# A graph network kernel on one core: the per-block sum of the messages as four accumulating fp32 products, and two PSUM tiles of counts

## The reference, cut to what matters

```python
node_feat = _mlp(x, W_node, b_node, g_node, beta_node)
edge_feat = _mlp(edge_attr, W_edge, b_edge, g_edge, beta_edge)
row, col = (edge_index[0], edge_index[1])
message = jnp.concatenate([x[row], x[col], edge_feat], axis=1)
message = _mlp(message, W_msg, b_msg, g_msg, beta_msg)
agg = jax.ops.segment_sum(message, col, num_segments=node_feat.shape[0])
```

## Time and profile before

| | us |
|---|---|
| median of 3 runs | 7316.13 (7313.47 to 7316.51) |
| the profiled execution | 7323.68 |
| its span, first to last instruction | 7321.9 |
| stages ahead of the messages | 0 to 1038 |
| message stage (806 steps) | 1038 to 5786 |
| second layer | 5786 to 7322 |
| PE / PEld busy | 4880.8 / 3210.7 |
| DVE / ACT / POOL busy | 3897.1 / 4078.4 / 3954.9 |

### The profile page before, as it was taken

One profiled execution on the slowest core, in us unless ns is written; L12 is line 12 of the kernel. 1 busy time (PEld: TensorE's weight loads), 2 busy tenths in 40 slices (PEclk: granted clock), 3 DMA queues, 4 the chain that ended last, 5 costly groups with the idle time before them and its releaser, 6 DMA issues. The chain is left out here.

```text
span 7321.9 us, 118928 instructions
## 1 busy us (share of the span) xinstructions
PE 4880.8 (67%) x30928; PEld 3210.7 (44%) x30928; DVE 3897.1 (53%) x12333; ACT 4078.4 (56%) x8897; POOL 3954.9 (54%) x4115
## 2 busy tenths in 40 slices
PE   5454446666666666666666666666666788888888
PEld 4111113444444434444444444443444556666667
DVE  6666654544444544445544444544454556666665
ACT  4555535555555555555555555555555436666665
POOL 4666645555555555555555555555555535555552
PEclk9555557676666667776777676776676559999998
DMA  5333323333333333333333333333333224444444
GB/s 194 99 104 102 103 60 106 89 99 94 89 104 88 89 104 88 99 94 88 107 89 97 96 87 105 91 95 99 87 108 88 69 64 159 159 167 167 163 156 160
DMA packets 377177, 788.71 MB, mean 108 GB/s; under 512 B 156868, under 2 KB 224468, under 8 KB 360516
## 3 DMA queue, kind: packets, MB, share of 16 engines
q1 hardware_dynamic: 233364, 421.01, 17.7%
q0 software_dynamic: 125872, 170.41, 11.0%
q10 hardware_dynamic: 17280, 189.67, 6.5%
HBM read 533.30 MB, written 247.34 MB: 107 GB/s over the span
## 5 line engine op out<-in xcount | busy, mean ns | idle before, releaser
L978 POOL DMA_INDIRECT gbuf<-a_tab,src_i x2688 | 2605.7, 969 | 2149.0 <-DVE pre L1078 1335.1
L1078 DVE TENSOR_TENSOR pre<-psum,gbuf 128x384 f32<-128x384 f32 x806 | 449.2, 557 | 2298.2 <-remote 1394.4
L1202 ACT ACTIVATE x_all<-psum 128x588 bf16<-128x588 f32 x1260 | 837.5, 665 | 1458.1 <-remote 861.8
L1189 PE MATMUL psum<-x_all 128*128 128x294 bf16 x2520 | 712.4, 377 | 1306.0 <-ACT x_all L1202 595.6
L1065 PE MATMUL psum<-rhs,lhs 128*128 128x96 f32 x6448 | 1230.8, 352 | 0.0
L1065 PEld LDWEIGHTS psum<-rhs,lhs 128*128 128x128 f32 x6448 | 1106.3, 258 | 0.7
L1109 PE MATMUL psum<-msg,oh 128*128 128x388 f32 x1612 | 991.3, 709 | 0.0
L1943 POOL DMA_INDIRECT sq<-t_tab,src_i x704 | 684.1, 972 | 532.0 <-PE psum L1999 380.8
L1189 PEld LDWEIGHTS psum<-x_all 128*128 128x128 bf16 x2520 | 225.4, 118 | 1580.2 <-issue 980.0
L1119 ACT ACTIVATE x_all<-psum 32x97 f32<-32x97 f32 x3224 | 770.1, 239 | 29.6 <-PE psum L1109 1.0
L1039 ACT ACTIVATE lhs<-psum,par 96x512 f32<-96x512 f32 x806 | 543.4, 674 | 305.0 <-remote 151.7
(11 more groups left out here) (234 smaller groups left out, 7427.0 us busy)
## 6 DMA issues: line engine op xcount, KB each, us to landing
adj_tab<-x_all ACTq DMA_DIRECT2D x120, 1543.5 KB
x_all<-adj_tab SPq DMA_DIRECT2D x60, 945.0 KB
nf<-adj_tab SPq DMA_DIRECT2D x60, 882.0 KB
gbuf<-a_tab,src_i POOLq DMA_INDIRECT x3224
x_all<-dst_row SPq DMA_DIRECT2D x806, 64.0 KB
gbuf<-adj_tab SPq DMA_DIRECT2D x60, 756.0 KB
lhs<-adj_tab SPq DMA_DIRECT2D x60, 504.0 KB
x_all<-attr_parts SPq DMA_DIRECT2D x807, 36.0 KB
```

Source lines behind the costliest of these rows:

```text
L978: g.indirect_dma_start(gbuf[:, k % 4, t, :], None, a_tab[:, :], bass.IndirectOffsetOnAxis(ap=src_i[:, first + t:first + t + 1], axis=0)).t ...
L1189: ins = pe.matmul(bank[6 + b][:, 0:HB], low_e[:, n % 2, :], key_e[:, n % 2, b * HB:(b + 1) * HB], start=True, stop=True)
L1202: act.activation(stage[:, :, j * SLOT:(j + 1) * SLOT].rearrange("p (b h) s -> p b h s", b=2), counts.rearrange("p b (h s) -> p b h s", s=S ...
```

## The change

The three parts of the sum by target become one. `sum_edges` is now four small fp32 products, one per tile of 128 edges, that accumulate in PSUM: the messages of the tile (97 columns) are the weights, its one-hots (32 columns) move. They write what `fold_blocks` wrote, to the same place (bank 2 + k%2, columns 384 to 415). `keep_blocks`, `fold_blocks`, `diag` and `sel` go. In PE's step the sum stands where the fold stood, ahead of the message product, and takes the block four steps back; `add_window` also moves from six steps back to four, and its wait for the message product from block k+4 to k+2.

Banks 4 and 5 are free by this. They become a second tile of counts: tile n goes to banks 4 and 5 or 6 and 7 in turn and waits for the copy of tile n-2. The one-hots of the counts become a ring of three, so DVE waits for the product of tile n-3 and no longer n-2.

```diff
@@ -954,10 +954,11 @@
         def ps_s(k):
-            return bank[4 + k % 2][:, 0:SUP * (C + 1)]
-
-        def ps_f(k):
             return bank[2 + k % 2][0:C + 1, SUP * C:SUP * C + W]
+
+        def ps_e(n):
+
+            return psum[:, (4 + 2 * (n % 2)) * 512:(6 + 2 * (n % 2)) * 512].rearrange("p (b f) -> p b f", b=2)[:, :, 0:HB]
@@ sum_edges
             pe.wait_ge(m_ok.sem, m_ok.at(MT * i + k))
             pe.wait_ge(oh_ok.sem, oh_ok.at(MT * i + k))
-            pe.wait_ge(d_ok.sem, d_ok.at(MT * i + k - 2))
-            pe.matmul(ps_s(k), oh[:, k % 4, :, :].rearrange("p t w -> p (t w)"),
-                      msg[:, k % 2, :, :].rearrange("p t c -> p (t c)"), start=True, stop=True).then_inc(s_mm.sem, 1)
-
-        def keep_blocks(act, i, k):
...
-        def fold_blocks(pe, i, k):
...
+            pe.wait_ge(s_add.sem, s_add.at(MT * i + k - 2))
+            for t in range(SUP):
+                ins = pe.matmul(ps_s(k), msg[:, k % 2, t, :], oh[:, k % 4, t, :], start=(t == 0), stop=(t == SUP - 1))
+            ins.then_inc(s_mm.sem, 1)
@@ add_window
-            dve.wait_ge(f_mm.sem, f_mm.at(MT * i + k))
-            dve.wait_ge(m_mm.sem, m_mm.at(last_message(MT * i + k + 4)))
+            dve.wait_ge(s_mm.sem, s_mm.at(MT * i + k))
+            dve.wait_ge(m_mm.sem, m_mm.at(last_message(MT * i + k + 2)))
@@ early_onehots
-            if n >= 2:
-                dve.wait_ge(n_mm, n - 1)
+            if n >= RING:
+                dve.wait_ge(n_mm, n - RING + 1)
@@ early_counts
-            if n:
-                pe.wait_ge(n_ok, n)
+            if n >= 2:
+                pe.wait_ge(n_ok, n - 1)
@@ PE's step
                         edge_product(pe, i, k)
                         early_counts(pe, MT * i + k, 0)
-                        fold_blocks(pe, *msgs.earlier(i, k, 6))
+                        sum_edges(pe, *msgs.earlier(i, k, 4))
                         message_product(pe, *msgs.earlier(i, k, 2))
                         early_counts(pe, MT * i + k, 1)
-                        sum_edges(pe, *msgs.earlier(i, k, 4))
@@ ACT's and DVE's steps
-                        keep_blocks(act, *msgs.earlier(i, k, 5))
...
-                        add_window(dve, *msgs.earlier(i, k, 6))
+                        add_window(dve, *msgs.earlier(i, k, 4))
```

More of the change, by code:

```diff
@@ L903, in gnn_kernel @@
         s_mm = signal("s_mm", 4)
-        d_ok = signal("d_ok", 2)
-        f_mm = signal("f_mm", 2)
         s_add = signal("s_add", 2)
[L907 to L910, removed]
+        RING = 3
+        X1 = 2 * ES + 2 * C
         HI = N // P + 1
@@ L914, in gnn_kernel @@
         NE = d.NE
-        X1 = X0 + W + 2 * (C + 1)
         X2 = X1 + (NE * GT + 1) // 2
         X3 = X2 + HI * QS // 2
-        X4 = X3 + KW
-        X5 = X4 + P
+        X4 = X3 + RING * KW // 2
+        X5 = X4 + RING * P // 2
         rel_e = x_flat[:, X1:X2].bitcast(BF16)[:, 0:NE * GT].rearrange("p (n j) -> p n j", j=GT)
         stage = x_flat[:, X2:X3].bitcast(BF16).rearrange("p (h s) -> p h s", h=HI)
-        iota_e = x_flat[:, X3:X4]
-        key_e = x_flat[:, X3:X4].bitcast(BF16).rearrange("p (b f) -> p b f", b=2)
-        low_e = x_flat[:, X4:X5].bitcast(BF16).rearrange("p (b f) -> p b f", b=2)
+        iota_e = x_flat[:, X3:X3 + KW]
+        key_e = x_flat[:, X3:X4].bitcast(BF16).rearrange("p (b f) -> p b f", b=RING)
+        low_e = x_flat[:, X4:X5].bitcast(BF16).rearrange("p (b f) -> p b f", b=RING)
         iota_ke = x_flat[:, X5:X5 + HB].bitcast(F16)
@@ L1174, in early_onehots @@
             e, j, n = tile
[L1175 to L1178 removed]
+            if n >= RING:
+                dve.wait_ge(n_mm, n - RING + 1)
+            dve.tensor_scalar(key_e[:, n % RING, :], iota_ke, keys[:, e % 2, j:j + 1], None, ALU.is_equal)
+            dve.tensor_scalar(low_e[:, n % RING, :], iota_le, lows[:, e % 2, j:j + 1], None, ALU.is_equal).then_inc(n_oh, 1)
         def early_counts(pe, k, second):
@@ L1200, in early_keep @@
                 act.wait_ge(o_adj, 32 * e)
-            counts = psum[:, 6 * 512:8 * 512].rearrange("p (b f) -> p b f", b=2)[:, :, 0:HB]
             act.activation(stage[:, :, j * SLOT:(j + 1) * SLOT].rearrange("p (b h) s -> p b h s", b=2),
-                           counts.rearrange("p b (h s) -> p b h s", s=SLOT), ACT.Copy).then_inc(n_ok, 1)
+                           ps_e(n).rearrange("p b (h s) -> p b h s", s=SLOT), ACT.Copy).then_inc(n_ok, 1)
         def early_store(act, k):
@@ L1400, in _ @@
                 def _(pe):
-                    for x in (r_mm, m_mm, s_mm, f_mm):
+                    for x in (r_mm, m_mm, s_mm):
                         x.start(pe)
-                    pe.wait_ge(sel_ok, 1)
                     for b in range(STREAMS):
@@ L1413, in step @@
                         early_counts(pe, MT * i + k, 0)
-                        fold_blocks(pe, *msgs.earlier(i, k, 6))
+                        sum_edges(pe, *msgs.earlier(i, k, 4))
                         message_product(pe, *msgs.earlier(i, k, 2))
                         early_counts(pe, MT * i + k, 1)
-                        sum_edges(pe, *msgs.earlier(i, k, 4))
-                    msgs.run(pe, step, 6)
+                    msgs.run(pe, step, 4)
                 @block.scalar
                 def _(act):
-                    for x in (r_ok, m_ok, m_sq, d_ok):
+                    for x in (r_ok, m_ok, m_sq):
                         x.start(act)
@@ L1430, in step @@
                         square(act, *msgs.earlier(i, k, 3))
-                        keep_blocks(act, *msgs.earlier(i, k, 5))
-                    msgs.run(act, step, 5)
+                    msgs.run(act, step, 3)
                     act.wait_ge(o_adj, 32 * NE)
@@ L1438, in _ @@
                     dve.memset(acc[:, :, :], 0.0).then_inc(m0, 1)
-                    dve.tensor_reduce(sel, ident[:, :].rearrange("p (t w) -> p w t", w=W), AX, ALU.add).then_inc(sel_ok, 1)
                     dve.wait_ge(m0, 2)
@@ L1464, in step @@
                         early_onehots(dve, MT * i + k + 1, 1)
-                        add_window(dve, *msgs.earlier(i, k, 6))
+                        add_window(dve, *msgs.earlier(i, k, 4))
                         onehot(dve, *msgs.earlier(i, k, 1))
-                    msgs.run(dve, step, 6)
+                    msgs.run(dve, step, 4)
         with nc.Else():
```

17 lines of the change are left out of this document (2 added, 15 removed).

## The result

The changed kernel takes 7575.68 us (median of 4 runs, 7572.94 to 7580.85) and the kernel before 7314.8 us beside it (4 runs, 7310.54 to 7316.51). The ratio is 1.0358, with a 95% interval from 1.034 to 1.0376: 3.6% slower, +261 us where +188 was forecast.

The account below looks back on a forecast made before the run. Bound: `pre` waits behind gathers, and the DVE-PE chain in free steps. 241 steps x 0.78 us = +188, other terms 0; 7323.7 + 188 = 7512, less 7.5 for the median of runs: 7504 us, range 7205 to 7670.

Parts of the forecast that it names:

- The two bounds: Message stage: `pre` held behind POOL's gathers, and in free steps the chain DVE to PE and back, 4.65 us a step.
- The held rounds of eight gathers: Message stage: two steps take 13.0 us whatever PE does, the second `pre` starting 1.8 us after POOL's row ends.
- The price of four products: On PE ahead of the message product: 1.37 us at 1.2 GHz, 0.69 at 2.4; net of the fold +0.96 and +0.48.
- The rival by which each product costs more than its load: On PE: the four products cannot overlap, each part costing 0.25 or 0.13 us; +350 us, 7666; chance 0.13.
- the yielding hold: Rival: waits behind the gathers come from PE's semaphores or waits and shorten by a tenth; -139 us, 7177; chance 0.13.
- the estimate of +118 us: On PE: by the skill's load rule, six more loads cost 0.49 us at either clock, times 241 steps.
- the old sum: On PE behind the message product, 1.43 us at 1.2 GHz, 0.74 at 2.4: removal gives only longer idle time.
- ACT's copies: On ACT, four copies of 243 ns a step go: counted as nothing, at most 68 us.
- the wait for ACT's copy: PE's counts waited 595.6 us in 189 times; removal by the second counts tile counted 0, far end -80 us.
- The rival of PE's throughput: PE's work, not its chain, ends last in free steps: 0.39 us x 269 steps = -105 us, 7211; chance 0.13.
- How many steps pay: Message stage: mean of 214 and 269, so 241 steps at 0.78 us, +188 us; ends +55 and +608.
- PE busy time down by some 200 to 300 us: Sign expected in the profile after: PE's busy time falls by this much without a gain in time.

Follow-up runs that it names:

- one-tile kernel: The changed kernel with a single PSUM tile of counts, each product waiting for the copy of the tile before: 6611.8 us, 1.1623 against the kernel before on that chip.
- the old place with 32 columns: The changed kernel with its four products moved behind the message product, where the wide sum stood, and one tile of counts: 5958.76 us, 1.047 against the kernel before.
- the chain cut in the changed kernel: The changed kernel with DVE making the next step's first one-hots ahead of `pre`, not behind it: 6091.45 us, 1.072 against the kernel before.
- with 128: Four products behind the message product, one tile of counts, each streaming its 32 one-hot columns four times over: 5667.09 us, 0.9974 against the kernel before.

## Why the prediction was right, and where it was off

**The two bounds were the right ones.** The held rounds of eight gathers are 13.0 us as forecast, with `pre` 1.3 us behind POOL's row (1.8 forecast), and the loss is outside them.

**The price of four products** was read from the fold's loads: 1.37 us at 1.2 GHz, measured 1.40. (The split of the fold's 0.41 us into 0.25 and 0.16 is not in those rows; a finer view of the same loads has 0.24 and 0.17.) The step was to be 5.6 us and is 5.63. The rival by which each product costs more than its load is out, and so is the yielding hold. The Trainium skill (TensorE: Matmul & The Clock Gate, LDWEIGHTS) gives a load's time by its columns alone; for 97 columns that is an estimate of 0.081 us. The trace does not agree at 1.2 GHz: the eight loads lie 1.40 / 8 = 0.175 us apart, and the estimate of +118 us is less than half of the +261 measured. The rows decided rightly.

**Off the chain, nothing.** The forecast gave nothing for the old sum, for ACT's copies and for the wait for ACT's copy (596 us in 189 times). The trace agrees: that wait went, and PE's wait for the one-hots grew by 243 times and 494 us. The one-tile kernel agrees too, but it ran without the hold, where there was next to no such wait to remove; with the hold this point rests on the waits alone. The rival of PE's throughput is out too: in the free steps PE is idle for 0.87 us, as before.

**How many steps pay, and at which clock.** This is the mis-sized term. "38% of its time is at 2.4 GHz and the mean is 0.62 x 0.96 + 0.38 x 0.48 = +0.78 us" takes the clock as given, but the change moved it: 0.50 throughout. A step that had stood at 1.2 GHz lost 5.63 - 4.65 = 0.98 us, against the 0.96 forecast. One that had run at 2.4 GHz is in DVE's timeline of the kernel before:

```profile
3552.75 0.56 DVE L1078 TENSOR_TENSOR pre<-psum,gbuf 128x384 f32<-128x384 f32 x1 [0.77 <-PE psum L1065]
3556.18 0.56 DVE L1078 TENSOR_TENSOR pre<-psum,gbuf 128x384 f32<-128x384 f32 x1 [0.37 <-PE psum L1065]
```

Its 3.43 us became 5.63, and of those 2.2 us the clock took 4.65 - 3.43 = 1.22. The two short steps of six were to lose 2 x 0.78 = 1.56 us and lost 2.37, and 0.35 came in the step before them. Against it, 0.85 came back in the held step behind. That is the held round once more: before the change 100 of the 209 rounds began with the second of the two short steps, so that this step was often not free, and its loss was taken in. The forecast's price per step was too low and its number of paying steps too high, and the two misses pull against each other: 1.94 us in six steps against 241 x 0.78 / 134 = 1.40. With the measured loss of a short step and all the rest the same, the sum would have been a little too high: 241 x 2.37 / 2 = +286. That +188 came as near to +261 as it did is in part luck.

**"PE busy time down by some 200 to 300 us"** was wrong for the same reason: 582 us up in the stage.

**What stays open.** The stages above show that the clock is lower with the narrow streams; the mechanism behind it was not tested. How much of the 3.6% is the clock's and how much the place's was not measured with the hold: the products at the old place with 32 columns and the chain cut in the changed kernel ran only without it. How the hold comes about is open too (below).

## What to carry to other kernels

- Before a product is replaced by several small ones, ask where on the chain they stand. Work that moves from behind a product to the front of it is paid for in full while the consumer waits, even if it is less work: here 0.47 us less per step on PE, and 0.98 us more per step in time.
- The clock is part of the cost. Ask what a change of shapes does to it, not only to the engine's busy time: with four products of 32 columns the stage ran at 0.50, with the same four at 128 columns at 0.85.
- Before a wait is removed because it is large (596 us here), look for what comes next on the same engine. And where DVE makes what PE waits for behind something that PE also feeds, try the order first: two lines on DVE gave more than the whole change (1.3% faster).

## What the runs showed of the hardware that was not expected

**The clock and the stream's width.** A PE busy for 97% of a stage stayed at 0.50, one busy for 75% was granted 0.85. The nearest pair is the old place with 32 columns (0.50, PE busy for 94%) and with 128 (0.85, busy for 75%). The kernels differ only in the width of the stream and of what it writes, and they ran on two chips with nearly the same time before.

**The hold and the chip.** The same kernel took 5681 and 5688 us on two chips, 7233 us on a third, and 7315 us in the first comparison. On the slower ones a `pre` waits for a remote cause behind rows of gathers; on the faster ones the list of waits has no such line. With the gathers left out, a slower chip ran the stage in 3120 us. The rest of that run, outside the stage, took 5687 - 3120 = 2567 us, where the unchanged kernel on a chip without the hold has 5683 - 3445 = 2238; the other stages kept their gathers, so they may be held too, which was not tested. The hold needs the gathers and something else that differs between these runs. It stayed the same through all runs on a chip, but no chip was measured at two times, so whether it belongs to the chip or to the time is open. One consequence was measured: the same change costs 16.7% without the hold and 3.6% with it. A change's worth in one such place is not its worth in the next, and even the bound is another one (POOL's 1.25 us per gather without the hold).
